# Starting the second block's scores inside the first block's last batches in a fused two-layer decoder kernel

## What is computed

```python
# block 0: linear attention, 16 heads of 16, 64 features
q, k, v = heads(x @ Wqkv + bqkv)
qf, kf = exp(q @ omega - |q|^2/2), exp(k @ omega - |k|^2/2)
out = (qf @ (kf^T @ v)) / (qf @ sum(kf) + 1e-6)
x = layernorm(x + out @ Wout + bout)
# block 1: cross-attention to the text, 16 heads of 16, then an MLP
q, k, v = x @ Wq + bq, ctx @ Wk + bk, ctx @ Wv + bv
out = softmax(q k^T / 4) @ v
x = layernorm(x + relu(out @ W1 + b1) @ W2 + b2)
# block 2: 8 experts, top 2, capacity 140; then layer 1
```

## Time and profile before

| what | value |
|---|---|
| runs: median (lowest to highest), 3 runs | 1127.52 us (1127.37 to 1131.48) |
| the profiled execution: its time | 1125.14 us |
| its span, first to last instruction | 1123.3 us |
| mean granted TensorE clock of the span | 0.934 |
| first scores on PE (start of stage 1's units on PE) | 96.5 us (107.3 us) |

### The profile page before, as it was taken

One profiled execution on the slowest core, in us unless ns is written; L12 is line 12 of the kernel. 1 busy time (PEld: TensorE's weight loads), 2 busy tenths in 40 slices (PEclk: granted clock), 3 DMA queues, 4 the chain that ended last, 5 costly groups with the idle time before them and its releaser, 6 DMA issues.

```text
span 1123.3 us, 22133 instructions
## 1 busy us (share of the span) xinstructions
PE 968.8 (86%) x8864; PEld 700.9 (62%) x8864; DVE 676.0 (60%) x1576; ACT 591.4 (53%) x1390; POOL 291.2 (26%) x305
## 2 busy tenths in 40 slices
PE   7997878888779998999898688888888888978997
PEld 4664556666458885566666556666666566645755
DVE  3346545455849965656566477766767766539302
ACT  4632556444348965454554355455546545567444
POOL 3521332000240005212112131221221222337344
PEclk9997899769889999999999899999899899989999
DMA  9350545400668977452252243313213202100001
GB/s 317 106 92 22 122 109 81 116 12 1 204 208 309 315 262 257 151 175 88 96 180 97 71 129 112 104 35 121 77 62 112 56 1 99 71 1 1 1 1 33
DMA packets 66679, 123.72 MB, mean 110 GB/s; under 512 B 11632, under 2 KB 41968, under 8 KB 62496
## 3 DMA queue, kind: packets, MB, share of 16 engines
q1 hardware_dynamic: 64528, 117.48, 34.4%
q0 software_dynamic: 2048, 4.82, 1.4%
HBM read 86.30 MB, written 35.92 MB: 109 GB/s over the span
## 4 chain that ended last, share of the span: by engine, by line
PE 52%; DVE 22%; ACT 12%; DMA 6%; issue 4%; POOL 3%; SPq 1%; POOLq 0%; DVEq 0%; ACTq 0%
PE psum L413 36%; ACT s_p L2803 4%; DVE s_p L2845 3%; DVE s_max L2834 2%; DMA raw_wd<-in_wd 2%; PE psum L2762 2%; PE psum L2773 2%; PE psum L1410 2%; DVE s_pT L2826 1%; PE psum L2236 1%; DVE junk L1930 1%; PE psum L2946 1%; PE psum L568 1%; DVE s_max L687 1%; DMA ctx_raw<-in_ctxT 1%
## 5 line engine op out<-in xcount | busy, mean ns | idle before, releaser
L2803 ACT ACTIVATE s_p<-psum,s_max 112x375 f32<-112x375 f32 x128 | 72.1, 568 | 98.3 <-DVE s_max L2834 98.3
L734 POOL TENSOR_TENSOR rstd<-meanvar,minus_half 112x1 f32<-112x1 f32 x40 | 25.7, 643 | 245.4 <-DVE meanvar L679 172.0
L687 DVE TENSOR_REDUCE s_max<-psum 112x2 f32<-112x750 f32 x64 | 59.5, 936 | 37.5 <-PE psum L568 36.5
L2762 PE MATMUL psum<-ident,s_p 112*125 112x112 f32 x384 | 62.6, 295 | 9.4 <-DVE s_p L2845 4.5
L2834 DVE TENSOR_REDUCE s_max<-psum 112x1 f32<-112x375 f32 x128 | 63.7, 539 | 2.1 <-PE psum L2754 1.9
L2754 PE MATMUL psum<-s_k,s_q 64*112 64x375 f16 x384 | 46.7, 349 | 19.3 <-ACT s_p L2803 7.4
L2762 PEld LDWEIGHTS psum<-ident,s_p 112*125 112x125 f32 x384 | 51.0, 197 | 19.8 <-DVE s_p L2845 6.8
L413 PE MATMUL psum<-Wv,ctx 128*125 128x512 f16 x240 | 59.8, 400 | 3.4 <-issue 2.6
L3200 POOL TENSOR_TENSOR rs<-ms,minus_half 112x32 f32<-112x32 f32 x8 | 43.5, 5437 | 70.8 <-DVE ms L3128 70.8
L413 PE MATMUL psum<-ctx,Wk 128*128 128x375 f16 x320 | 60.6, 324 | 0.0
L1472 ACT ACTIVATE s_pT<-psum 125x672 f32<-125x672 f32 x64 | 46.6, 729 | 22.3 <-PE psum L1398 20.9
(11 more groups left out here) (403 smaller groups left out, 2488.4 us busy)
## 6 DMA issues: line engine op xcount, KB each, us to landing
keys<-s_k SPq DMA_DIRECT2D x64, 187.5 KB, 2.3
s_k<-keys SPq DMA_DIRECT2D x8, 1500.0 KB, 7.7
values<-s_v SPq DMA_DIRECT2D x48, 224.0 KB
s_v<-values SPq DMA_DIRECT2D x16, 672.0 KB
raw_wg<-in_wg SPq DMA_DIRECT2D x8, 1024.0 KB, 6.7
raw_wu<-in_wu SPq DMA_DIRECT2D x8, 1024.0 KB, 7.1
raw_wd<-in_wd SPq DMA_DIRECT2D x8, 1024.0 KB, 7.7
s_kd<-k_halves SPq DMA_DIRECT2D x48, 93.8 KB, 3.8
```

What stands on the lines that cost most here:

```text
L687: VE.tensor_reduce(s1_max[b % 2][:, 2 * p:2 * p + 2], rings["s1"][unit][0:N, :, 0:S], X, ALU.max, negate=True).then_inc(*V.up("max1", n))
L2762: ins = TE.transpose(rings["t4"][unit][0:SCH, c * N:(c + 1) * N], p[:, c * SCH:(c + 1) * SCH], ident[0:N, 0:N])
L2803: SC.activation(rings["p4"][2 * n + j], rings["s4"][(n, j)][0:N, 0:S], ACT.Exp, bias=s4_max[b % 2][:, h:h + 1], accum_out=s4_sum[b % 2][:, ...
```

## The change

It lets `s0_queries` place the first scores once `attT0` of batches 0 to 3 is placed (not 7); batches 4 to 7 become streams of their own (`late`), which ask for 2 free banks where the others ask for 3, take one bank at a time for `num0`, share the four banks left after the scores have taken theirs, and go on in stage 1 if they are not done. The fences between stage 0 and stage 1 go; single waits on `num0` of batches 0 to 3 stand in for them. To make room, half of stage 0's tiles lie where `raw0` was, so `raw0` is loaded in stage 1 once `norm` of batches 4 to 7 is placed and PE has done `attT0` of them. `Wv4` is loaded at the head of stage 1, the `split` units come 3 batches of `st1` later, and block 1's `bias` is a stream of its own, ahead of the text load.

```diff
@@ qget
             sp.wait_ge(L_qx["qx", b], T["feat0", 1, H // 2 - 1])
+            if b == 2:
+                sp.wait_ge(*first_batches())
@@ tiles
+    later_half = Region(nc, ringm.base + 24 * KB, 24 * KB)
+    k_f = [r.tensor(f"k_f{i}", [P, 4, HALF]) for i, r in enumerate((work, later_half))]
+    q_feat = [r.tensor(f"q_feat{i}", [P, H // 2, HALF]) for i, r in enumerate((work, later_half))]
@@ s0_batch, for b >= NB0 = 4
-        yield from until_free("misc0", 3)
+        yield from until_free("misc0", 3 if b < NB0 else 2)
...
+        else:
             yield from until(("turn0", b - 4))
+            for odd in range(2):
+                yield from until_free("misc0", 3 if b < NB0 else 2)
+                yield [("num0", b, odd)]
+                yield from rest(REST / 2)
+                yield [("num0e", b, odd)]
+                yield from rest(REST / 2)
@@ s0_queries
+    def s0_late(first):
+        yield from until(("num0", first - NB0, 1))
+        yield from s0_batch(first)
...
         yield from s1_queries(0)
         yield from rest(4 * REST)
-        yield from until(("attT0", B - 1))
+        yield from until(*(("attT0", b) for b in range(NB0)))
         ring = rings["misc0"]
-        while any(name not in r.value for j in range(4) for r, name in ring.freed[j]):
-            yield None
+        for j in range(4):
+            while any(name not in r.value for r, name in ring.freed[j]):
+                yield None
+            ring.turn.remove(j)
...
-    weave(follow(s0_features, (0, 1)), *(s0_batch(b) for b in range(B)),
-          s0_keys(), s0_queries())
+    late = [s0_late(b) for b in range(NB0, B)]
+    weave(follow(s0_features, (0, 1)), *(s0_batch(b) for b in range(NB0)),
+          s0_keys(), s0_queries(), also=late)
@@ sync_s0
-        for j, (n, _, _) in enumerate(MATS):
-            SY.dma_start(raw0[j][:], a[n][0]).then_inc(*L_exp[j].up("expert", 0, j))
@@ stage 1's plan
-    rings.update(o1=banks(4, 1),
-                 misc1=banks(5, 3), pT1=Ring(s1_pT))
+    rings.update(o1=pass_one(rings["misc0"]), misc1=rings["misc0"], pT1=Ring(s1_pT))
...
+    def s1_bias(b):
+        yield from until(("norm", 0, b), ("v1", b, 0))
+        yield [("bias", 1, b)]
...
     def s1_split():
+        yield [("wv4in",)]
+        yield from until(*(("norm", 0, b) for b in range(NB0, B)))
+        yield [("raw0in",)]
         for j in range(3):
-            yield from until(("st1", (j + 2) * HP - 1))
+            yield from until(("st1", (j + 5) * HP - 1))
             for half in range(2):
                 yield [("split", 0, j, half)]
-        place(("wv4in",))
-        yield from until(("st1", 6 * HP - 1))
-        yield [("wv4",)]
+            if j == 0:
+                yield [("wv4",)]
...
-          follow(s1_queries, range(2, B, 2)))
+          follow(s1_queries, range(2, B, 2)), follow(s1_bias, range(B)), *late)
@@ every engine's part of stage 1 (here PE's)
-        fence(pe, 1)
         for unit in plans[1]:
             what, *at = unit
-            if what == "v1":
+            if of_block0(unit):
+                tensor_unit0(unit)
+            elif what == "v1":
@@ sync_s1
-        fence(sp, 1)
         for what, *at in plans[1]:
             if what == "wv4in":
                 g_wv4.start()
+            elif what == "raw0in":
+                sp.wait_ge(*(T["attT0", b] for b in range(NB0, B)))
+                for j, (n, _, _) in enumerate(MATS):
+                    SY.dma_start(raw0[j][:], a[n][0]).then_inc(*L_exp[j].up("expert", 0, j))
```

More of the change, by code:

```diff
@@ L204, in build, with weave @@
     hurry = [False]
-    def weave(*streams, filler=iter(())):
-        live, passed = list(streams), 0
-        while live:
+    def weave(*streams, filler=iter(()), also=()):
+        live, passed = [*streams, *also], 0
+        while any(stream not in also for stream in live):
             for stream in list(live):
@@ L927, in s0_batch @@
         yield [("out", 0, b)]
-        yield from norm_and_turn(0, b, free=3)
+        yield from norm_and_turn(0, b, free=3 if b < NB0 else 2)
     def s0_keys():
@@ L1000, in build, with of_block0 @@
         place_ctx(i)
-    weave(follow(s0_features, (0, 1)), *(s0_batch(b) for b in range(B)),
-          s0_keys(), s0_queries())
+    late = [s0_late(b) for b in range(NB0, B)]
+    weave(follow(s0_features, (0, 1)), *(s0_batch(b) for b in range(NB0)),
+          s0_keys(), s0_queries(), also=late)
     end_stage()
+    UNITS0 = ("kf0", "v0", "kvT0", "kvT0e", "kv0", "kv0e", "num0", "num0e", "turn0", "turn0e",
+              "attT0", "attT0e")
+    def of_block0(unit):
+        return unit[0] in UNITS0 or unit[:2] == ("out", 0)
```

457 lines of the change are left out of this document (239 added, 218 removed).

## The result

The changed kernel takes 1147.12 us (median of 4 runs, 1144.08 to 1148.13) against 1129.5 us for the kernel before beside it; the ratio is 1.0144, 95% interval 1.01 to 1.0189. A second set on another chip gave 1147.97 us (6 runs) against 1127.22, ratio 1.0191 (1.0127 to 1.0255). It is slower, by 17.6 and 20.7 us in the medians, where no change was forecast and 1136 was the upper end of the range. The profiled execution took 1144.08 us, span 1142.3, granted clock 0.928.

What follows compares the result with a forecast made beforehand. PE leads; tight are queries to first score and text load to batch 3's keys. Stage 1 earlier -1.4, bias -0.7, load +2.0 sum to -0.1 us: 1125.0 profiled, median 1127.4, against 1127.52; range 1118 to 1136.

Steps and rivals of the forecast that it cites:

- The queries: Stage 0, ahead of the first score: the queries come 2.3 us earlier, bounds 0 and 3.6.
- The first score: Placed 3 to 4 us of work behind q1; PE stands about 4.3 us (0 to 7.8), score at 92 to 95.
- What the stand costs: DVE before stage 1: 3.3 us run during the stand, 12.6 left at 92.9, through at 106.2; barrier had ended at 107.3.
- Rival C: PE stands at first score, clock falls (sign: below 0.6 until stage 1): +4 to +6, about 1132; chance 0.15.
- The barrier and four banks: Between stages 0 and 1: stage 1 begins 1.4 us earlier, 1.1 of it from the stand's sum; banks 0 (up to 4.4).
- The bias: Stage 1, chain between text load and keys: bias goes earlier on POOL, 0.7 us gained.
- The memset: Start of stage 1: ACT's wait of 1.64 us for POOL's memset goes, at nothing.
- The expert's load: Stage 1, SP's queue ahead of qput and batch 3's text load: 2.0 us lost, bounds 0 and 7.5.
- The splits: Stage 1: six ACT copies of 1.05 us move later and cost 0, between a gain of 1 and a loss of 1.
- B: Load's 7.5 us fall right ahead of batch 4's text load or batch 3's gets: +5.5 to +7, about 1134; chance 0.17.

Runs made afterwards that it cites:

- b3: Kernel before with only the splits moved later (39th, 47th, 55th pair, Wv4's between): 1136.6 us, ratio 1.0101.
- d7: Kernel before plus a pause of 40 chained small DVE copies (8.3 us) at the end of stage 1: 1138.6 us, ratio 1.0101.
- b1: Kernel before with only the looser gate (first scores wait for attT0 of batches 0 to 3): 1134.1 us, ratio 1.0075.
- a1: Changed kernel with the gate undone (first scores wait for attT0 of all eight batches): 1132.0 us, ratio to before 1.008.
- a5: Changed kernel with the barrier between the blocks put back on all five engines: 1146.7 us, ratio to before 1.0191.
- e4: Changed kernel with gate and splits undone, expert loads at about 95 us, memset behind the first queries' put, and the barrier put back: 1121.0 us, ratio to before 0.9974.
- a13: Changed kernel with two parts undone, gate (scores wait for all eight batches) and splits (placed where they were): 1128.6 us, ratio to before 1.0035.
- e1: Changed kernel with gate and splits undone and the first expert's loads issued after the last attT0, about 95 us: 1123.6 us, ratio to before 0.9982.
- b2: Kernel before with only the first expert's loads moved from the start of SP's queue to behind the first mput: 1133.5 us, ratio 1.0089.
- a3: Changed kernel with the splits of the first expert's weights and of Wv4 placed as in the kernel before: 1130.4 us, ratio to before 1.006.
- a2: Changed kernel with the first expert's loads issued only after the sixteenth pair's exponentials: 1143.2 us, ratio to before 1.015.
- e3: Changed kernel with gate and splits undone, expert loads at about 95 us, POOL's memset waiting for x_tok of batch 3: 1120.3 us, ratio to before 0.9961.

## Why the prediction was wrong

**The queries** came earlier on PE by 1.0 us (85.38 against 86.34), not 2.3. The term was over-sized, and its sign isn't shown: b3 and d7, with the stage 0 of the kernel before, have this `q1` at 85.91 and 84.08. From it to score 8 these three took 21.0 to 21.7 us, the kernel after 28.5, b1 26.3 and a1 22.0, so the losses at the entry are clear of this spread.

**The first score** stood as forecast: placed a few us of work behind `q1`, PE idle 5.22 us (4.3 was the estimate), first score at 93.80 (92 to 95).

**What the stand costs** is the first step that failed. It said that 3.3 us of DVE's work can run during the stand, that 12.6 us are left at 92.9, and that these are done with 0.7 us idle at 106.2, since DVE had been busy for 10.13 of 10.8 us before. That took a share of one order of work for a property of the work. During the stand DVE did nothing (0.00 of 5.22 us), since what it could have done waited for units behind the score in PE's list; only one `turn0e` had come before. From 92.9 to 115.42 DVE was busy for 17.67 us, 2.2 of which are the stall beside the memset, and idle for 4.85. So 15.4 us were left instead of 12.6, and 4.85 us were idle instead of 0.7; with the stall that is the 9.2 us by which DVE was through later than forecast. Most of the idle time, 3.9 us, lies before 100.2: 1.5 until the first score was made, then 1.25 and 1.03 in waits for PE, which worked at half the clock (0.50). The rounds of 2.36 us that follow are not a loss: the clock is back at 0.98 and DVE is busy for 9.61 of 10.10 us. `mT1` came at 115.47 instead of near 106. Alone on the kernel before (b1) score 8 is 5.1 us later, undone in the kernel after (a1) 6.6 us earlier. Rival C had the place, the stand and the half clock, and named DVE's waits for it; its sign, under 0.6 up to stage 1, held only to 100 us, and it had no term for the DVE work that the stand itself puts off. How much of the 6.6 us is the clock and how much the order no run parts.

**The barrier and four banks** were right at about nothing, as far as can be measured. a5 and e4 put the barrier back without a change that can be measured, and with four banks kept a1, a13 and e1 reach score 8 at 107.1 to 107.8. **The bias** left the chain between text and keys, as said; the 0.7 was not measured alone.

**The memset** I costed at nothing because only ACT's wait for it was looked at the earlier trace rows. It held up DVE's `x_tok` for 2.2 us, on the chain.

**The expert's load** is the second failed step: the mechanism was right, the size was not. 2.0 was taken between 0 and 7.5; from score 8 to 24 it costs 4.7 us in the kernel after (38.0 against 33.3) and 5.8 in b2, and 5 us of median between a13 and e1. The text load landed 6.85 us after its issue, 8.0 in b2, and 3.8 with the queue empty. The queries' put just ahead of it landed 6.38 us after its issue instead of 2.04, some 4.3 us late. When it was issued, at 122.51, one of the three loads had just landed (122.49), the second landed at 124.98, and the third, at 2.5 us each, by estimate near 127.5; so nearly all that was left of them came first. The Trainium skill's rule in "DMA: Bandwidth & Descriptors", section "Queues, rings and completion order" (each engine takes a ring's descriptors in order), by which the delay would be all that is left of the 7.5 us, was the better guide. I had weighed it as agreeing and then taken 2.0.

**The splits** are the third failed step: "they cost what they did, in a stretch with the same loop: 0". It looked at ACT's six copies and not at the low halves on DVE, which the same stream yields after the last of them. In the kernel before these too come behind the last score's maximum (245.14), but at once and in one run, ahead of DVE's work of the tail:

```profile
246.49 2.35 DVE L1372 SCALAR_TENSOR_TENSOR wg<-raw_wg,wg 128x1024 f16<-128x1024 f32 x2
...
256.92 1.21 DVE L423 SCALAR_TENSOR_TENSOR Wv<-w_Wv,Wv 64x1024 f16<-64x1024 f32 x1
```

With the last split behind pair 55 (on ACT at 254.5) they fall between the last batches' norms, 6 us behind the last maximum (246.59) and up to 25:

```profile
252.86 2.35 DVE L1426 SCALAR_TENSOR_TENSOR wg<-raw_wg,wg 128x1024 f16<-128x1024 f32 x2
...
270.25 1.21 DVE L425 SCALAR_TENSOR_TENSOR Wv<-w_Wv,Wv 64x1024 f16<-64x1024 f32 x1
```

Tail 56.4 against 48.8 (a3), 59.9 in b3, 5.5 us at equal clock; median 9 us over the kernel before by b3, 17 under the kernel after by a3. The step moved six units and forgot the seven queued behind them in the same stream.

**Adding up.** In stage 1 the three are 6.6 + 4.7 + 7.6 = 18.9 us at their own places in the kernel after. Undone one by one they gave 15, 4 (a2, which paid elsewhere) and 17 in the median, two together 19, all three 24 (e1). So the parts are not additive in the total. These differences are between runs on several chips; taken from the ratios to the kernel before beside each, a1 gave 7 to 12 us, a3 10 to 15, a13 18 and e1 18 to 24. And the 18.9 us are differences to the undone parts: against the one profile before, stage 2 begins 7.5 and 10.6 us later (294.5 and 297.6 against 287.0). With b1, b2 and d7 for the stretch that this profile took slowly, the kernel before would begin stage 2 near 280, an estimate (107.3 + 33.3 + 139), and 14 to 18 of the 20 us lie ahead of it. No case of the prediction held more than one loss at a time: B, at 1134, was the outermost. Of the three only the load's 4.7 lay inside the bounds I had given it (0 to 7.5); the entry was bounded at a loss of 2 and the splits at 1.

**What stays open** is the rest. Stages 2 to 6, the same code with the same 6271 PE instructions, took 824.6 us before, 836.1 and 840.4 after, and 821 to 838 in the others. Busy time in that stretch, first the kernel before, then after (columns as in the earlier trace rows):

```profile
287.00:1111.60 824.60, 725.06 (x6271) 529.37 (x6272) 525.30 (x1217) 451.28 (x1107) 217.86 (x200) 0.95 0.36 116
```

```profile
294.50:1130.60 836.10, 734.73 (x6271) 534.22 (x6272) 524.91 (x1217) 451.98 (x1107) 219.33 (x200) 0.94 0.35 114
```

DVE, ACT and POOL agree within 1.5 us, PE is busy 9.7 us longer at a granted clock of 0.94 instead of 0.95. Over all 131 runs of the kernel before the time falls as the mean granted clock rises, from 1135 us at 0.926 to 1115 at 0.945, and the runs of the changed kernel lie at 0.922 to 0.934. But b1, e1 and e4 took 836.8, 838.3 and 837.4 us in these stages too, with PE busy for 735.4, 732.9 and 731.6, and e1 and e4 are no slower than the kernel before. So long later stages do not belong to the changed kernel alone, and single profiles can't say how much of the 20 us they are. That they explain why a1 moved the total by more than its place shows is likely, not shown; the one experiment on it (d7) was too coarse.

## What to carry to other kernels

When a step is moved in a planned order, follow the whole stream it belongs to and every queue it enters: the cost here lay in what came after the moved work in the same stream (the low halves) and behind it in the same queue (the text load). A bulk load belongs where DMA is idle and no chain of small transfers is about to start, and a first use of data placed too near its request blocks an engine that works in order, with everything behind it. And a share of busy time only bounds a stretch as long as the order of the work stays the same.

## What the hardware showed

POOL's memset to SBUF and DVE's fp32 `x_tok` (SBUF to SBUF) did not run together: 2.65 us instead of 0.41 at 110.0 and at 100.3 us, 3.49 instead of 0.89 for two at 82.2, and normal again once the memset was kept from them (e3). Work of DVE that reads PSUM wasn't slowed: `s_q` took 0.45 beside it, and the maxima in the kernel before 0.94. The Trainium skill has the rule in "SBUF — State Buffer", section "SBUF: two separate sides": DVE in a two-port mode and GpSimd share a port pair that whoever starts first holds for the whole instruction. The traces agree, and `x_tok` waited through both memsets in a row; that it ran in such a mode no trace shows.

A profile of one execution is coarser than its digits: identical code from score 24 to 60 took 87.6 and 92.1 us, and runs of the kernel before lay between 1113.7 and 1141.5 us on four chips, in step with the granted clock.
